# Index bits of a table look-up: GpSimd comparisons and subtractions replaced by VectorE int32 and-operations

## The chip, the core and the metric

One program runs on one core of a Trainium2 chip. The core's engines run side by side, each through its own list of instructions in order: TensorE (PE; its weight loads are shown apart as PEld), VectorE (DVE), ScalarE (ACT), GpSimd (POOL), and SyncE (SP), which here only issues DMAs. They are held together by semaphores: an instruction may wait until a semaphore has reached a number, and may raise one when it ends. The metric is the device time of the whole program in microseconds (us), lower being better.

## What is computed

Four layers of attention and feed-forward blocks run over activations of 4 batches x 256 rows x 256 columns. The change lies in the third layer (numbered 2), whose feed-forward block holds its weights as indices into a table of 16 numbers:

```python
def _ghost_linear(x, idx, lut):
    w = lut[idx]                      # lut: 16 floats, idx: int32 from 0 to 15
    return jnp.einsum('bsh,oh->bso', x, w)
gate = _ghost_linear(x, gate_idx, lut)    # 688 x 256 indices
up   = _ghost_linear(x, up_idx, lut)      # 688 x 256
...
return _ghost_linear(h, down_idx, lut)    # 256 x 688
```

Before it comes that layer's cross attention: 16 heads of width 16, 4 batches of 256 queries, keys split into main and extra ones. The kernel computes the weights `w = lut[idx]` of the feed-forward block while this attention runs.

## The kernel before

**The look-up.** All indices of the layer lie in one tile `w2` (in `regD`) of 128 partitions x 4288 words, loaded as int32 and replaced in place by float weights. It is cut into 8 pieces (`LUT_PIECES`) of LP = 536 words. For each piece the index b3 b2 b1 b0 is split into bits, and a binary tree of selections is walked:

- GpSimd (lines 593 to 607) turns the int32 indices into floats (`left`, line 601), then for 8, 4 and 2 writes a mask m = bit if left >= bit else 0 (line 603) and subtracts it (line 604). What is left is b0 as a float (`lut_b0`). That is 7 instructions a piece and 56 in all, each waiting for the one before (`link`). Two sets of buffers alternate, so piece i waits until the 7 selections of piece i - 2 are done (`lut_pick`). It signals `lut_bits`.
- ScalarE (`lut_leaves`, lines 954 to 963) makes 8 leaves lut[2k] + b0 (lut[2k+1] - lut[2k]), two instructions in each of four steps k. Each step waits for `lut_bits`, later ones also for selections that free a buffer. It signals `lut_leaf`. The first leaf is written over the indices in `w2`.
- VectorE (`lut_step`, lines 1605 to 1625) selects between leaves with 7 predicated copies (`choose`, line 1611), by m1 (bit 2), m2 (bit 4) and m3 (bit 8).

**Where it sits.** The attention runs over b = 0 to 3 and h = 0 to 15; I number its 64 steps i = 16 b + h. In a step TensorE forms the shifted scores of head i (lines 2207 and 2208), the plain scores of a head of the next batch (line 2187, in steps h = 3 to 12 of b = 0 to 2), and the values of head i - 1 (line 2223). Both scores of a head are written to one of two banks, so TensorE's line 2187 waits until VectorE has taken the row maxima of the head two before. VectorE takes these maxima (lines 1573 and 1574), ScalarE the exponentials (line 977), VectorE normalises four heads at a time (lines 1592 to 1598) in steps h = 2, 6, 10, 14. Once in a batch VectorE splits the 32 maxima of each head and row into three bf16 parts (lines 1581 to 1584) for TensorE's line 2194, which ScalarE copies out (line 952).

**The order** is written by hand. Piece p of the look-up has seven steps; its step s stands in attention step i = 5 + 7 p + s (`LUT_START, LUT_STEPS = 5, 7`). ScalarE makes leaves in steps 1 to 4, VectorE selects in steps 2 to 6, so step 0 is empty on both engines. In VectorE's list the look-up stands behind the maxima of the same attention step and ahead of the normalising. GpSimd has nothing else to do between the layer norms before and behind the attention (`ln_pow`, lines 449 to 452). The feed-forward block behind the attention, `ffn(1)`, waits for all 56 selections.

## Time and profile before

| | us |
|---|---|
| median of 3 runs | 1039.76 |
| lowest and highest | 1039.58 and 1040.32 |
| the profiled execution | 1043.5 |
| its span in the trace | 1042.0 |

The profile is of one execution. Its times count from the span's start, and the attention with the look-up lies between 708 and 866 us. An instruction's duration runs from its start to its end; on one engine the next one may start a little before the end of the one before, when it waits for nothing.

| profile of the stretch 700 to 866 us | |
|---|---|
| predicated copies of the look-up (VectorE, line 1611) | 56, busy 54.08 us |
| leaves of the look-up (ScalarE, line 962) | 64, mean 0.82 to 0.83 us |
| GpSimd's masks and subtractions (lines 603, 604) | 24 and 24, median 2.0 and 1.3 us |
| granted TensorE clock, mean | 0.89 |

### The profile page before, as it was taken

The numbers are of one execution on the slowest core, as the hardware profiler recorded it, in microseconds if no ns is written. First come the engines' busy times: TensorE is split into PE (matmuls) and PEld (weight loads), VectorE is DVE, ScalarE is ACT, GpSimd is POOL, SyncE is SP. The second block draws the span as 40 slices with busy tenths as digits, with TensorE's granted clock in tenths as the row PEclk, the third lists the DMA queues.
The fourth block names the chain that finished last, engine by engine and source line by source line (L and its number), as shares of the span: only waits on it lengthen the run. The fifth ranks groups of instructions, "written<-read, shape, count | busy, mean of one in ns | idle before, by whom it ended". The sixth has DMA issues, their size and how long they took to land.

```text
span 1042.0 us, 13075 instructions
## 1 busy us (share of the span) xinstructions
PE 875.7 (84%) x4352; PEld 618.7 (59%) x4352; DVE 719.4 (69%) x1377; ACT 533.1 (51%) x983; POOL 444.4 (43%) x274
## 2 busy tenths in 40 slices
PE   5795999999999997645669896958688799999998
PEld 3354777787787776423344553727477685545646
DVE  5247789989899997689856757745989873353311
ACT  2485687787777877622312524535587572112120
POOL 2011678878788785654630002005467540600000
PEclk8898899999999998966869998967699999999999
DMA  4003000000000000003120000000000001200000
GB/s 124 16 6 131 16 17 22 23 15 15 15 15 30 18 1 6 1 0 157 39 82 0 1 1 0 1 1 1 1 2 2 1 1 35 94 0 1 11 10 21
DMA packets 12923, 24.25 MB, mean 23 GB/s; under 512 B 4280, under 2 KB 8656, under 8 KB 11728
## 3 DMA queue, kind: packets, MB, share of 16 engines
q1 hardware_dynamic: 12448, 20.53, 6.0%
q10 hardware_dynamic: 432, 3.15, 0.8%
q8 instruction: 26, 0.43, 0.2%
q14 instruction: 17, 0.14, 0.0%
HBM read 22.63 MB, written 1.05 MB: 23 GB/s over the span
## 4 chain that ended last, share of the span: by engine, by line
PE 30%; DVE 17%; issue 5%; ACT 4%; POOL 1%; ACTq 0%; DVEq 0%
PE PS L2120 12%; PE PS L2169 6%; PE PS L2223 3%; DVE mxf L1573 2%; DVE regD L1611 1%; PE PS L2024 1%; PE PS L1673 1%; DVE regB L1611 1%; DVE regA L1323 1%; PE PS L2000 1%; DVE mx_am L1274 1%; PE PS L2187 1%; PE PS L2038 1%; PE PS L2207 1%; PE PS L1946 1%
## 5 line engine op out<-in xcount | busy, mean ns | idle before, releaser
L483 POOL TENSOR_TENSOR X<-X,xn 128x512 f32<-128x512 f32 x64 | 108.1, 1689 | 75.7 <-ACT xn L701 75.0
L451 POOL TENSOR_SCALAR veps<-mv 128x4 f32<-128x4 f32 x16 | 5.5, 346 | 266.7 <-DVE mv L1023 266.7
L1122 DVE TENSOR_TENSOR_SCAN regB<-regB 128x1024 f32<-128x1024 f32 x32 | 84.4, 2641 | 0.2
L1103 DVE TENSOR_SCALAR_CACHE_REDUCE regA<-PS,nrq 128x256 bf16<-128x256 f32 x128 | 56.0, 475 | 38.0 <-PE PS L1748 36.1
L720 ACT ACTIVATE regA<-PS,nb,rq 128x256 f32<-128x256 f32 x128 | 72.0, 574 | 13.5 <-DVE regA L1103 12.7
L2223 PE MATMUL PS<-regA 128*128 128x128 f32 x512 | 74.8, 293 | 3.4 <-ACT regA L977 3.3
L477 POOL TENSOR_TENSOR y<-y,regB 128x1024 f32<-128x1024 f32 x32 | 75.5, 2362 | 3.9 <-DVE regB L1133 3.8
L1770 PE MATMUL PS<-regA 128*128 128x256 f32 x256 | 67.6, 387 | 7.3 <-DVE qss L1090 7.2
L2223 PEld LDWEIGHTS PS<-regA 128*128 128x128 f32 x512 | 68.2, 206 | 7.1 <-ACT regA L977 6.1
L1779 PE MATMUL PS<-regA 128*128 128x256 f32 x256 | 68.4, 391 | 1.1 <-ACT xn L701 1.1
L1748 PE MATMUL PS<-regA 128*128 128x256 f32 x256 | 68.3, 390 | 0.0
L1721 PE MATMUL PS<-xnT,regA 128*128 128x512 f32 x128 | 60.6, 616 | 4.6 <-ACT regA L692 3.4
L2120 PE MATMUL PS<-xnT,regB 128*128 128x512 f32 x128 | 61.1, 628 | 1.3 <-ACT xnT L632 1.3
L2169 PE MATMUL PS<-regB 128*128 128x256 f32 x256 | 58.7, 387 | 3.6 <-DVE X L1550 3.5
L916 ACT ACTIVATE regB<-PS 128x512 f32<-128x512 f32 (+1 forms) x28 | 16.7, 596 | 84.1 <-PE PS L2120 84.0
L2120 PE MATMUL PS<-regA,regB 128*128 128x512 f32 x128 | 55.8, 594 | 1.4 <-ACT regA L906 1.4
L701 ACT ACTIVATE xn<-PS,ls 128x256 f32<-128x256 f32 x128 | 54.3, 487 | 5.0 <-DVE ls L1109 2.4
L2169 PEld LDWEIGHTS PS<-regB 128*128 128x128 f32 x256 | 49.2, 194 | 12.6 <-DVE X L1550 4.3
L1770 PEld LDWEIGHTS PS<-regA 128*128 128x128 f32 x256 | 47.5, 193 | 14.7 <-DVE qss L1090 8.4
L1779 PEld LDWEIGHTS PS<-regA 128*128 128x128 f32 x256 | 50.2, 197 | 8.7 <-issue 1.4
L1748 PEld LDWEIGHTS PS<-regA 128*128 128x128 f32 x256 | 46.5, 195 | 14.8 <-issue 9.6
L726 ACT COPY regA<-PS 128x512 f32<-128x512 f32 x64 | 38.0, 595 | 29.6 <-PE PS L1759 29.6
(271 smaller groups left out, 2164.4 us busy)
## 6 DMA issues: line engine op xcount, KB each, us to landing
regA<-in_W SPq DMA_DIRECT2D x16, 384.0 KB, 3.0
regB<-in_wg SPq DMA_DIRECT2D x2, 1024.0 KB, 6.3
regB<-in_wu SPq DMA_DIRECT2D x2, 1024.0 KB, 8.4
X<-in_x SPq DMA_DIRECT2D x1, 1024.0 KB, 7.8
regC<-in_wg ACTq DMA_DIRECT2D x1, 1024.0 KB, 5.7
regC<-in_wu ACTq DMA_DIRECT2D x1, 1024.0 KB, 7.9
regC<-in_wd ACTq DMA_DIRECT2D x1, 1024.0 KB, 9.9
regB<-in_wd SPq DMA_DIRECT2D x1, 1024.0 KB, 9.0
```

What stands on the lines that cost most here:

```text
L477: pool.tensor_tensor(halves(y3, i), halves(y3, i), halves(prod, i), ALU.add).then_inc(y_done, 1)
L483: pool.tensor_tensor(xt, xt, xh0[b % 2], ALU.add).then_inc(x0_add, 1)
L720: act.activation(p0[i][:, q, :], bank(S_BANK + i)[:, q * S:(q + 1) * S], ACT.Exp, bias=nb0[:, i, q:q + 1], scale=rq[par][:, 2 * b + q:2 * ...
L1103: ins = dve.tensor_scalar(spill[:, i, q, :], bank(S_BANK + i)[:, q * S:(q + 1) * S], nrq[par][:, t:t + 1], None, ALU.mult, ALU.min, accum_ ...
L1122: dve.tensor_tensor_scan(v(hs), v(dA), v(dBu), 0.0, ALU.mult, ALU.add).then_inc(scan_done, 1)
L1721: last = pe.matmul(to[:, i * HALF:(i + 1) * HALF], w0[par][:, c * P:(c + 1) * P], xnT[:, c, i * HALF:(i + 1) * HALF], start=c == 0, stop=c ...
L1748: last = pe.matmul(bank(S_BANK + b % 2)[:, q * S:(q + 1) * S], qT[par][:, (2 * b + q) * P:(2 * b + q + 1) * P], kT[par][:, b * S:(b + 1) * S],
L1770: last = pe.matmul(bank(O_BANK)[:, 0:S], ctxN[:, 2 * b + k, :], pT0[b % 2][:, k, :], start=k == 0, stop=k == 1)
L1779: last = pe.matmul(bank(W_BANK)[:, q * DIM:(q + 1) * DIM], oT0[b % 2][:, q * P:(q + 1) * P], wvo[par], start=True, stop=True)
L2120: last = pe.matmul(bank(to)[0:rows, :], w[:, k, c * P:c * P + rows], src[:, k, :], start=k == 0, stop=k == KD - 1)
L2169: last = pe.matmul(bank(6 + td % 2)[:, 0:DIM], hT[0:rows, c, t * P:(t + 1) * P], wd[0:rows, c, :], start=c == 0, stop=c == nch - 1)
L2223: last = pe.matmul(bank(6 + g % 2)[:, at:at + P], pT2[i % 3][:, k, q * P:(q + 1) * P], V2flat[:, v:v + P], start=k == 0, stop=k == 1)
```

## The change

GpSimd's loop goes away whole. The formerly empty step 0 of each piece on VectorE gets four instructions that read the int32 indices and write the bits 2, 4, 8 and 1 as int32, by `bitwise_and` with a constant. The masks are read as words that are zero or not, so an int32 2 serves as well as a float 2.0. ScalarE now reads b0 as int32 0 or 1 in place of a float. The three masks raise a semaphore of their own, `lut_mask`, for which the first selection waits; b0 raises `lut_bits`, for which ScalarE waits as before. The waits for free buffers move to VectorE's list.

```diff
-            pool.wait_ge(ld_i2, 16 * 5)
-            pool.wait_ge(stk_out, 4 * B)
-            for i in range(LUT_PIECES):
-                left = lut_b0[i % 2]
-                if i == 1:
-                    pool.wait_ge(q2_mm, 4)
-                if i >= 2:
-                    pool.wait_ge(lut_pick, 7 * (i - 1))
-                link(pool.tensor_copy(left, w2[:, i * LP:(i + 1) * LP].bitcast(I32)))
-                for m, bit in zip(lut_m[i % 2][::-1], (8.0, 4.0, 2.0)):
-                    link(pool.tensor_scalar(m, left, bit, bit, ALU.is_ge, ALU.mult))
-                    ins = pool.tensor_tensor(left, left, m, ALU.subtract)
-                    if bit > 2:
-                        link(ins)
-                ins.then_inc(lut_bits, 1)
...
-                    last = act.activation(dst, lut_b0[i % 2], ACT.Identity, scale=lutd[:, leaf:leaf + 1], bias=lut[:, 2 * leaf:2 * leaf + 1])
+                    last = act.activation(dst, lut_b0[i % 2].bitcast(I32), ACT.Identity, scale=lutd[:, leaf:leaf + 1], bias=lut[:, 2 * leaf:2 * leaf + 1])
...
             def lut_step(i, step):
 
                 A = w2[:, i * LP:(i + 1) * LP]
+                if step == 0:
+                    if i == 1:
+                        dve.wait_ge(q2_mm, 4)
+                    if i >= 2:
+                        dve.wait_ge(lut_pick, 7 * (i - 1))
+                    for m, bit in zip(lut_m[i % 2], (2, 4, 8)):
+                        dve.tensor_scalar(m.bitcast(I32), A.bitcast(I32), bit, None, ALU.bitwise_and).then_inc(lut_mask, 1)
+                    dve.tensor_scalar(lut_b0[i % 2].bitcast(I32), A.bitcast(I32), 1, None, ALU.bitwise_and).then_inc(lut_bits, 1)
...
-                        dve.wait_ge(lut_bits, i + 1)
+                        dve.wait_ge(lut_mask, 3 * i + 3)
```

Three places in the lists of instructions show what moves. Names such as regB or xnT are the large regions in which the tiles lie; `[waits ...]` names the semaphores. Line numbers behind line 590 are 15 lower in the changed kernel until line 1593, and 7 lower from the look-up's selections on (1611 becomes 1604).

VectorE at piece 1 (b = 0, h = 12 and 13), before: from the maxima of the last head to the first selection.

```order
L1573 TENSOR_REDUCE mxf<-PS 128x2 [waits s2_mm]
L1574 TENSOR_REDUCE mxf<-PS 128x2
L1581 CAST mxs<-mxf 128x2x32 [waits mx_tr,max2]
L1582 TENSOR_TENSOR mxr<-mxf,mxs 128x64 [waits dve_chain]
L1583 CAST mxs<-mxr 128x2x32 [waits dve_chain]
L1584 TENSOR_TENSOR mxs<-mxr,mxs 128x2x32 [waits dve_chain]
L1611 COPY_PREDICATED regD<-xnT,regC 128x536 [waits lut_leaf,lut_bits]
```

The same place in the changed kernel.

```order
L1558 TENSOR_REDUCE mxf<-PS 128x2 [waits s2_mm]
L1559 TENSOR_REDUCE mxf<-PS 128x2
L1599 TENSOR_SCALAR xnT<-regD 128x536 [waits q2_mm]
L1599 TENSOR_SCALAR xnT<-regD 128x536 x2
L1600 TENSOR_SCALAR regC<-regD 128x536
L1566 CAST mxs<-mxf 128x2x32 [waits mx_tr,max2]
L1567 TENSOR_TENSOR mxr<-mxf,mxs 128x64 [waits dve_chain]
L1568 CAST mxs<-mxr 128x2x32 [waits dve_chain]
L1569 TENSOR_TENSOR mxs<-mxr,mxs 128x2x32 [waits dve_chain]
L1604 COPY_PREDICATED regD<-xnT,regC 128x536 [waits lut_leaf,lut_mask]
```

The four and-operations now stand between the last maxima and the split of the maxima. The same four stand at piece 3 (b = 1, h = 10) between maxima and normalising: first before, then after.

```order
L1573 TENSOR_REDUCE mxf<-PS 128x2
L1574 TENSOR_REDUCE mxf<-PS 128x2
L1592 RECIPROCAL rl<-PS 128x16
L1596 TENSOR_TENSOR regC<-PS,rl 128x2x64
L1597 TENSOR_TENSOR regC<-PS,rl 128x128
```

```order
L1558 TENSOR_REDUCE mxf<-PS 128x2
L1559 TENSOR_REDUCE mxf<-PS 128x2
L1599 TENSOR_SCALAR xnT<-regD 128x536 x3
L1600 TENSOR_SCALAR regC<-regD 128x536
L1577 RECIPROCAL rl<-PS 128x16
L1581 TENSOR_TENSOR regC<-PS,rl 128x2x64
L1582 TENSOR_TENSOR regC<-PS,rl 128x128
```

GpSimd, before: the end of the layer norm ahead of the attention, and the first of eight such pieces.

```order
L451 TENSOR_SCALAR veps<-mv 128x4
L452 TENSOR_TENSOR rstd<-veps,neghalf 128x4
L601 CAST regD<-regD 128x536
L603 TENSOR_SCALAR regB<-regD 128x536
L604 TENSOR_TENSOR regD<-regD,regB 128x536
L603 TENSOR_SCALAR regB<-regD 128x536
L604 TENSOR_TENSOR regD<-regD,regB 128x536
```

In the changed kernel GpSimd goes straight from one layer norm to the next, with nothing in between.

## Rows read from the trace of the kernel before

**Rows 1.** The page: busy time by engine, then the span in 40 slices.
```profile
PE 875.7 (84%) x4352; PEld 618.7 (59%) x4352; DVE 719.4 (69%) x1377; ACT 533.1 (51%) x983; POOL 444.4 (43%) x274
...
DVE  5247789989899997689856757745989873353311
```

**Rows 2.** Waits, 690 to 870 us: who waited for whom, us in total, times, longest.
```profile
PE PS L2187 <- DVE mxf L1574: 24.8, 18, 4.9
PE PS L2194 <- DVE mxs L1584: 6.2, 4, 2.1
ACT regA L977 <- PE PS L2208: 28.4, 23, 6.5
DVE mxf L1573 <- PE PS L2187: 13.7, 11, 4.7
```

**Rows 3.** Chain that ended last, 680 to 880 us: start, us, what (pieces picked out).
```profile
732.76 1.75 DVE regD L1611
...
754.25 0.88 DVE mxs L1581
...
793.01 1.89 DVE regD L1611
...
807.22 1.86 DVE regD L1611
...
841.29 1.84 DVE regB L1611
843.15 1.04 DVE regD L1611
```

**Rows 4.** GpSimd's two operations by line: duration in ns (min/median/max), first and last start.
```profile
L603 POOL TENSOR_SCALAR regB<-regD x12: 2003/2014/2580, 710.3 to 824.5; 128x536 f32<-128x536 f32 x12
L604 POOL TENSOR_TENSOR regD<-regD,regB x12: 1316/1322/1328, 712.4 to 827.0; 128x536 f32<-128x536 f32 x12
```

**Rows 5.** VectorE's predicated copies (line 1611) alone: stretch, length, busy (count), PEclk.
```profile
700.00:866.00 166.00, 54.08 (x56) 0.89 0.00 1
```

**Rows 6.** Timeline of VectorE, then of GpSimd: start us, us, what.
```profile
790.93 0.61 DVE L1581 CAST mxs<-mxf 128x64 bf16<-128x64 f32 x1
...
792.21 0.77 DVE L1611 COPY_PREDICATED regB<-xnT,regC 128x536 f32<-128x536 uint32 x1
793.01 1.88 DVE L1611 COPY_PREDICATED regD<-xnT,regB 128x536 f32<-128x536 uint32 x1
...
790.36 2.51 POOL L603 TENSOR_SCALAR regB<-regD 128x536 f32<-128x536 f32 x1
792.96 1.32 POOL L604 TENSOR_TENSOR regD<-regD,regB 128x536 f32<-128x536 f32 x1
```

**Rows 7.** Int32 and-operations of VectorE elsewhere by line, then its start-to-start spacing (timeline).
```profile
L1178 DVE TENSOR_SCALAR regA<-regC x6: 672/673/674, 149.0 to 370.1; 128x1024 int32 x6
L1275 DVE TENSOR_SCALAR mx_am<-mx_am x10: 180/181/1695, 454.2 to 519.6; 128x32 int32<-128x32 int32 x10
...
693.36 0.65 DVE L1573 TENSOR_REDUCE mxf<-PS 128x2 f32<-128x480 f32 x1
693.93 0.18 DVE L1574 TENSOR_REDUCE mxf<-PS 128x2 f32<-128x32 f32 x1
```

**Rows 8.** Timeline of ScalarE at pieces 1, 2 and 7: start us, us, what [idle before].
```profile
753.03 0.83 ACT L962 ACTIVATE regD<-regC,lut,lutd 128x536 f32<-128x536 f32 x1
...
756.64 0.37 ACT L952 COPY regB<-PS 96x256 bf16<-96x256 bf16 x1 [1.57 <-PE PS L2194]
...
767.90 0.82 ACT L962 ACTIVATE regD<-regD,lut,lutd 128x536 f32<-128x536 f32 x1
...
849.83 0.82 ACT L962 ACTIVATE regD<-regC,lut,lutd 128x536 f32<-128x536 f32 x1
```

**Rows 9.** Timeline of VectorE where the and-operations land: start us, us, what [idle before].
```profile
753.47 0.65 DVE L1573 TENSOR_REDUCE mxf<-PS 128x2 f32<-128x480 f32 x1
...
803.04 0.66 DVE L1573 TENSOR_REDUCE mxf<-PS 128x2 f32<-128x480 f32 x1 [1.72 <-PE PS L2187]
...
818.93 0.69 DVE L1419 TENSOR_TENSOR X<-X,regC 128x512 f32<-128x512 f32 x1 [1.59 <-PE PS L2072]
...
839.43 0.90 DVE L1611 COPY_PREDICATED regD<-regB,regC 128x536 f32<-128x536 uint32 x1 [3.71 <-ACT regC L962]
```

**Rows 10.** Timeline of ScalarE in b = 2: the leaf ahead of the 811 us selection.
```profile
809.91 0.82 ACT L962 ACTIVATE regC<-regD,lut,lutd 128x536 f32<-128x536 f32 x1
```

More of the change, by code:

```diff
@@ L312, in build @@
                              "o2_norm", "co_tr", "coT_done", "wo2_mm", "wo2_add"))
-        lut_bits, lut_leaf, lut_pick, sx_done, z_done, z_tr, z_add, bf_done, hw_mm, wd3_done, hs3_done, xh_mm, xh_out = (
-            sem(n) for n in ("lut_bits", "lut_leaf", "lut_pick", "sx_done", "z_done", "z_tr", "z_add", "bf_done", "hw_mm", "wd3_done",
+        lut_bits, lut_mask, lut_leaf, lut_pick, sx_done, z_done, z_tr, z_add, bf_done, hw_mm, wd3_done, hs3_done, xh_mm, xh_out = (
+            sem(n) for n in ("lut_bits", "lut_mask", "lut_leaf", "lut_pick", "sx_done", "z_done", "z_tr", "z_add", "bf_done", "hw_mm", "wd3_done",
                              "hs3_done", "xh_mm", "xh_out"))
```

## The prediction

> **What bounds the kernel now.** I read the page first. TensorE is the busiest engine over the span, and GpSimd, from which the work is taken, the idlest of the four [rows 1]. Averages over the span say little here, so I turned to the stretch of the attention, 708 to 866 us. Its waits show a ring: TensorE's plain scores wait 24.8 us for VectorE's maxima and its line 2194 6.2 us for the split maxima, while ScalarE's exponentials wait 28.4 us for TensorE and VectorE waits 13.7 us for TensorE [rows 2]. No row of ScalarE or VectorE waits for GpSimd's bits. The chain of waits goes through VectorE in long runs from 727 to 836 us, and then through TensorE and ScalarE. VectorE is what paces b = 0 to 2, since there it has maxima for the next batch to take. In b = 3 it has none, and there ScalarE and TensorE pace.
>
> So GpSimd's loop is never waited for, and taking it off GpSimd is worth nothing by itself. The change is decided by what it does to VectorE, in two ways of opposite sign.
>
> **What is taken away: a slowing of VectorE.** The 56 selections are equal in size. Undisturbed ones take 0.75 to 0.77 us, but many take far more. At 793.01 one takes 1.88 us, having started 0.05 us behind a GpSimd subtraction of 1.32 us; the one at 792.21, beside a GpSimd mask operation, takes 0.77 [rows 6]. The excess of the first, 1.13 us, is close to the subtraction's length, 1.32 us in nearly all of its rows, while mask operations vary from 2.00 to 2.58 [rows 4]: the selection seems to wait until GpSimd's subtraction has finished. Together the 56 take 54.08 us [rows 5]; 56 x 0.757 is 42.4, so the excess is 11.7 us. Other small instructions are struck too: the cast at 754.25 takes 0.88 against 0.20 undisturbed [rows 3], that at 790.93 0.61 [rows 6], a third 0.30 too much, 1.4 us together.
>
> The Trainium skill, "SBUF — State Buffer", section "SBUF: two separate sides", says that VectorE instructions with two SBUF inputs and GpSimd ones that read SBUF take one port pair in turn, for a whole instruction. By that rule all of the excess ends with GpSimd's loop. It would also make a selection that starts beside a mask operation wait for its end, and the 0.77 us at 792.21 [rows 6] does not bear that out. If only the stretches at subtractions were the loop's doing, the sum below would have 1.3 us less of gain.
>
> How much of the excess lies on the chain? I went through it piece by piece. Six stretched selections are off it (759.53, 770.07, 794.79, 796.87, 839.43, 845.09), with 3.5 us of excess. The rest is 11.7 - 3.5 = 8.2 us of selections, from 732.76 to 843.15 [rows 3], and 1.4 us of casts: **9.6 us**. Not all of it will be passed on:
> - Around 807 us ScalarE works without a gap. The selection at 811.6 needs the leaf that starts at 809.91 and lasts 0.82 [rows 10], so it can't move ahead by all of the 1.86 us gained before it and only by about 0.9. I take 1.0 us off.
> - The last two, at 841.29 and 843.15 [rows 3], have 1.36 us of excess. ScalarE had waited for them only 0.61, so 0.75 comes off.
>
> **What is added: 32 and-operations on VectorE.** The kernel has such instructions elsewhere: int32 of 1024 columns takes 673 ns, of 32 columns 181 ns undisturbed [rows 7]. On the line between them 536 columns take 181 + 504 x 492 / 992 = 431 ns. Nothing is waited for between the four, and then VectorE starts the next instruction some 0.08 us before the end of the last (693.36 + 0.65 against 693.93) [rows 7]. A group of four is 3 x 0.35 + 0.43, less 0.08 at the end: **1.4 us**. Bounds are the two rows themselves, 4 x 0.1 and 4 x 0.6 us. All eight groups are 11.2 us of VectorE, about the 11.7 + 1.4 that it gets back. It is the places that decide:
> - Piece 0 (721.3 us) falls where VectorE soon waits 0.8 and then 2.8 us for TensorE: nothing.
> - Piece 1 stands behind the maxima of 753.47 [rows 9], with VectorE solid behind it: 1.4.
> - Piece 2 (767.2) has 0.85 us of VectorE's idle time behind it in three small gaps: 0.55.
> - Piece 3 (786.6) is in a solid run: 1.4.
> - Piece 4 (800.2) has the gap of 1.72 behind it, piece 5 (817.2) that of 1.59, piece 6 (835.7) that of 3.71 [rows 9]: nothing. The gaps are waits for TensorE or ScalarE; if those came earlier by as much as VectorE does, they would stay as they are.
> - Piece 7 (849.1) is in b = 3, where VectorE has time: nothing on VectorE.
>
> **What is moved: ScalarE now waits for VectorE.** The leaves of a piece need its bits. GpSimd had them ready long before; now they come from VectorE's list one attention step earlier, and VectorE is the engine that lags. At piece 1 the leaves start at 753.03 [rows 8], while the and-operations can't end before 754.1 + 1.4 = 755.5, or 754.5 after the 1.0 us gained at 732.76. ScalarE starts them 1.4 us late, has the 1.57 us of idle time ahead of 756.64 [rows 8] to take that up, and is held back behind it only through VectorE's split maxima; where it becomes the chain at 761 us, some 0.4 of the 0.6 us won there (1.4 added, 1.0 and 1.0 removed) is lost: 0.4. At piece 2 (leaves at 767.90, bits at 768.4) the lateness is within the 0.55 already counted. At piece 7 the bits come at 850.5, the leaf was at 849.83 [rows 8]; TensorE has an output projection of 1.7 us to do in between, which covers most of it, so I put down 0.2. At the others the bits are in time.
>
> ScalarE reads int32 now. No row of before shows that on ScalarE. Its operation runs at one column after another at 0.82 us whatever region it reads, and the nearest row with int32 on another engine, VectorE's, shows no extra cost [rows 7], so I take 0, with 64 x 0.1 us as the upper bound. The waits on `lut_pick` and `lut_mask` in VectorE's list are for its own, finished work: nothing. GpSimd's layer norm behind the attention is not held up by its loop before either, which ended at 846 us.
>
> **The sum.** -9.6 + 1.0 + 0.75 + 1.4 + 0.55 + 1.4 + 0.4 + 0.2 = -3.9 us, on the profiled execution's 1043.5. That one stands 3.7 above the median of the runs, of which nothing is due to this stretch; so on the median 1039.8 - 3.9 = **1035.9 us**. One thing is left to luck: the granted clock in this stretch averages 0.89 [rows 5], and falls after TensorE's idle times; the output projection at 815.9 us takes 2.99 where its like takes 1.73 at 850.6. One such fall more or less is 1.3 us.
>
> **The rivals.**
>
> *VectorE gives back more (1031).* The and-operations find gaps everywhere and the stretches return in full: -9.6 - 1.3 (one slow projection less) + 1.4 + 0.6 = -8.9. For it: the gaps behind pieces 4 to 6 did take their groups whole. Against: ScalarE has no gap around 762 to 775 and 801 to 811 us.
>
> *The gain is hidden (1039.3).* As VectorE speeds up, ScalarE with its 64 leaves of 0.82 and TensorE take over the pace at each stretch, and of 9.6 us only half is passed on, 4.8, against 4.3 us of costs: -0.5. For it: three engines are each busy for 70 to 90% of this stretch. Against: TensorE waited 31 us for VectorE in it [rows 2], which says that VectorE is the late one.
>
> *ScalarE waits for its bits (1043.5, slower).* The mechanism is VectorE's list: bits for piece p stand behind VectorE's backlog of step 5 + 7 p. By the times of the trace leaves would come 2.5 us late at piece 1, 0.7 at piece 2, 0.9 at piece 3 and 0.6 at piece 7, 4.7 us together; exponentials queue behind the leaves on ScalarE, and TensorE's values wait for these. If nothing takes that up, and half of the stretches is passed on, it is -4.8 + 3.4 + 4.7 + 0.4 = +3.7. It decides from the point where lateness exceeds ScalarE's slack ahead of its next wait, 1.57 us at piece 1. The same time would come of and-operations at the speed of a 512-column addition (0.69 us each), or of an int32 input that costs ScalarE 0.1 us each.
>
> *The change does not do what it says* would be stretches that stay with GpSimd silent; then VectorE only gains work, +3.4 to +4: it is in the chance of the slower case.
>
> **Chances.** Forecast 1035.9, with its own range of 1033 to 1038: 0.50. More given back: 0.11. Hidden: 0.18. Slower: 0.21. About 0.2%, 2.1 us, is what a measurement of this kernel can tell from no change. The forecast's range and the first rival are faster, 0.61; hidden is the same, 0.18; the last is slower, 0.21. The range that leaves out 0.2 runs from inside the first rival to inside the last: 1031.0 to 1042.5.
>
> **What would show it.** VectorE's selections all at 0.75 to 0.77 us, total about 42.5; and-operations at 0.43; VectorE's busy time in the stretch about the same as before. ScalarE's line 962 with waits for the and-operations of at most 2 us at pieces 1 and 2. TensorE's 24.8 us of waiting for maxima down by 3 or more. The forecast is wrong if the selections stay stretched, if ScalarE's leaves show waits of more than 4 us for the and-operations in total, or if they take longer with an int32 input.

## The result, and the profile after

| | before | changed |
|---|---|---|
| median of 10 runs, us | 1040.59 | 1034.82 |
| lowest and highest, us | 1039.19 and 1043.02 | 1033.01 and 1037.80 |
| ratio to before, 95% interval | | 0.9942 [0.9930, 0.9955] |
| profiled execution, its span, us | 1043.5, 1042.0 | 1034.1, 1032.5 |

The change makes the kernel faster by 5.8 us. The forecast was 1035.9 on 1039.8, a gain of 3.9 us. The time lies within the forecast's 1033 to 1038; 1.9 us of the gain were not foreseen, and the experiments below are mostly about them.

The page of the changed kernel, in answer to [rows 1]: 32 more instructions on VectorE and yet a little less busy time (716.0 us for 719.4); GpSimd lost 86.5 us.

```profile
PE 866.4 (84%) x4348; PEld 613.4 (59%) x4352; DVE 716.0 (69%) x1409; ACT 532.3 (52%) x983; POOL 357.9 (35%) x218
```

The and-operations by line: duration min/median/max in ns, first and last start. The forecast had 431 ns.

```profile
L1599 DVE TENSOR_SCALAR regB<-regD x12: 422/431/434, 718.2 to 828.3; 128x536 int32<-128x536 int32 x12
L1600 DVE TENSOR_SCALAR regC<-regD x4: 432/438/446, 751.1 to 839.7; 128x536 int32<-128x536 int32 x4
```

The selections alone, in the stretch of [rows 5]: stretch, length, busy and count, granted clock. They are down from 54.08 us to 42.46, 0.758 each. The clock of the stretch, the last number but two, rose from 0.89 to 0.94, for which the forecast had no term.

```profile
700.00:866.00 166.00, 42.46 (x56) 0.94 0.00 1
```

The waits of 690 to 870 us, as in [rows 2]: who waited for whom, us in total, times, longest.

```profile
PE PS L2180 <- DVE mxf L1559: 23.4, 19, 4.9
PE PS L2187 <- DVE mxs L1569: 5.4, 3, 2.3
ACT regA L962 <- PE PS L2201: 23.7, 22, 4.1
DVE mxf L1558 <- PE PS L2180: 12.0, 6, 5.4
```

TensorE's waits for maxima fell by 1.4 us only, where 3 or more were forecast. The longest wait of an exponential fell from 6.5 to 4.1 us.

**A better ruler than the whole time.** The first exponential starts between 704 and 710 us in the profiles of this study (708.7 and 707.4 in two of the kernel before, 705.7 and 706.8 in two of the changed one). From the start of the first exponential to that of the last, the same kernel repeats itself within 0.1 us. The exponentials by line, kernel before, then changed (first and last start stand behind the durations):

```profile
L977 ACT ACTIVATE regA<-PS x64: 572/592/617, 708.7 to 862.5; 128x512 f32<-128x512 f32 x64
```

```profile
L962 ACT ACTIVATE regA<-PS x64: 573/592/613, 705.7 to 853.1; 128x512 f32<-128x512 f32 x64
```

Before, 153.8 us; changed, 147.5. A second profile of each gave 153.8 and 147.5. Of the 9.5 us between the two spans 6.3 belong to the attention, and some 3 to an earlier start, which varies by as much between profiles and lies ahead of everything that the change touches. So the gain to be explained is **6.3 us** (the medians say 5.8, within the interval of 4.7 to 7.3). I call this distance the attention time, and the start of exponential i, counted from the first, its offset.

The offsets say where the gain arises. The forecast of each stretch is made of the terms of the sum, and of the excess of the selections that start in it.

| steps i | offset at its end, before | the same, changed | gain in it | forecast |
|---|---|---|---|---|
| to 32 (pieces 0 to 3) | 88.2 | 87.8 | 0.4 | 0.6 |
| 32 to 40 (piece 4) | 104.8 | 103.7 | 0.7 | 0.8 |
| 40 to 41 | 111.9 | 108.4 | 2.4 | 0.6 |
| 41 to 47 (piece 5) | 126.4 | 120.6 | 2.3 | 1.8 |
| 47 to 48 | 128.6 | 121.9 | 0.8 | 0 |
| 48 to 63 (pieces 6, 7) | 153.8 | 147.5 | -0.3 | 0.4 |

The selection at 811.60 counts from step 40 to 41, since the maxima that TensorE waits for there stand behind it. The forecasts add up to 4.2 rather than 3.9, since the single excesses on the chain come to 8.5 where I had taken the rest of the total, 8.2. Two single steps, 40 to 41 and 47 to 48, hold 3.2 us of gain, of which 0.6 was forecast. The rest agrees with the sum to within 0.7 us at each line.

### The profile page after: what moved, and what is told of

Its sections match the earlier page's. It is cut to its first block, busy times and chain, and to the rows that moved or that the text cites. A ratio compares the mean times of both kernels' runs of the same rounds, so it can differ in the third digit from the quotient of the medians.

```text
span 1032.5 us, 13046 instructions
## 1 busy us (share of the span) xinstructions
PE 866.4 (84%) x4348; PEld 613.4 (59%) x4352; DVE 716.0 (69%) x1409; ACT 532.3 (52%) x983; POOL 357.9 (35%) x218
## 3 DMA queue, kind: packets, MB, share of 16 engines
q10 hardware_dynamic: 432, 3.15, 0.8%
HBM read 22.63 MB, written 1.05 MB: 23 GB/s over the span
## 4 chain that ended last, share of the span: by engine, by line
PE 29%; DVE 17%; ACT 5%; issue 5%; POOL 1%; ACTq 0%; DVEq 0%
PE PS L2113 12%; PE PS L2162 6%; PE PS L2216 3%; DVE mxf L1558 2%; PE PS L1666 1%; PE PS L2017 1%; PE PS L1993 1%; DVE mx_am L1259 1%; DVE regA L1308 1%; PE PS L2031 1%; ACT regC L947 1%; DVE regA L1286 1%; PE PS L2180 1%; DVE xn L1017 1%; PE PS L2200 1%
## 5 line engine op out<-in xcount | busy, mean ns | idle before, releaser
L477 POOL TENSOR_TENSOR y<-y,regB 128x1024 f32<-128x1024 f32 x32 | 77.6, 2427 | 0.7 <-DVE regB L1118 0.6
L2216 PEld LDWEIGHTS PS<-regA 128*128 128x128 f32 x512 | 65.8, 200 | 6.9 <-ACT regA L962 5.8
L1763 PEld LDWEIGHTS PS<-regA 128*128 128x128 f32 x256 | 47.9, 194 | 14.8 <-DVE qss L1075 8.4
L1772 PEld LDWEIGHTS PS<-regA 128*128 128x128 f32 x256 | 50.3, 197 | 8.7 <-issue 1.4
L1741 PEld LDWEIGHTS PS<-regA 128*128 128x128 f32 x256 | 46.0, 193 | 14.6 <-issue 9.5
```

The source lines that it names most:

```text
L477: pool.tensor_tensor(halves(y3, i), halves(y3, i), halves(prod, i), ALU.add).then_inc(y_done, 1)
L1741: last = pe.matmul(bank(S_BANK + b % 2)[:, q * S:(q + 1) * S], qT[par][:, (2 * b + q) * P:(2 * b + q + 1) * P], kT[par][:, b * S:(b + 1) * S],
L1763: last = pe.matmul(bank(O_BANK)[:, 0:S], ctxN[:, 2 * b + k, :], pT0[b % 2][:, k, :], start=k == 0, stop=k == 1)
L1772: last = pe.matmul(bank(W_BANK)[:, q * DIM:(q + 1) * DIM], oT0[b % 2][:, q * P:(q + 1) * P], wvo[par], start=True, stop=True)
L2216: last = pe.matmul(bank(6 + g % 2)[:, at:at + P], pT2[i % 3][:, k, q * P:(q + 1) * P], V2flat[:, v:v + P], start=k == 0, stop=k == 1)
```

## What stands behind the two steps: TensorE's clock

TensorE of the kernel before, timeline: start us, us, what, idle time before it and its releaser.

```profile
815.52 0.38 PE L2187 MATMUL PS<-regA,regB 96*128 96x256 bf16 x2 [1.99 <-DVE mxf L1574]
815.74 3.15 PE L2072 MATMUL PS<-regC,regB 128*128 128x256 f32 x8
...
832.62 0.28 PE L2194 MATMUL PS<-identb,mxs 128*96 128x128 bf16 x2 [2.08 <-DVE mxs L1584]
...
834.90 1.91 PE L2223 MATMUL PS<-regA 128*128 128x128 f32 x8
```

Two stretches behind them (stretch, length, busy and count on PE, PEld, DVE, ACT, POOL, then the granted clock):

```profile
817.00:819.00 2.00, 2.00 (x7) 1.65 (x6) 0.41 (x3) 0.00 (x0) 1.91 (x2) 0.50 0.00 0
...
833.30:836.60 3.30, 3.30 (x17) 2.98 (x17) 2.32 (x6) 0.60 (x2) 1.70 (x2) 0.50 0.00 0
```

Line 2072 is the output projection, line 2223 the values of a head. Behind each wait of some 2 us the clock is at 0.50, that is 1.2 GHz; I call such a stretch a spell. The projection in the first takes 3.15 us, the eight matmuls of the values in the second 1.91. The same places in the changed kernel, timeline and stretches:

```profile
810.62 0.38 PE L2180 MATMUL PS<-regA,regB 96*128 96x256 bf16 x2 [1.25 <-DVE mxf L1559]
810.84 1.89 PE L2065 MATMUL PS<-regC,regB 128*128 128x256 f32 x8
...
824.52 0.28 PE L2187 MATMUL PS<-identb,mxs 128*96 128x128 bf16 x2 [1.21 <-DVE mxs L1569]
```

```profile
812.00:814.00 2.00, 2.00 (x17) 1.85 (x16) 2.00 (x7) 0.00 (x0) 0.00 (x0) 1.00 0.00 0
...
826.00:828.00 2.00, 2.00 (x20) 1.95 (x19) 1.93 (x7) 1.04 (x2) 0.00 (x0) 1.00 0.00 0
```

The waits are 1.25 and 1.21 us, the clock stays at 1.00 (2.4 GHz), the projection takes 1.89 us, and the values take 1.06 (at 826.02). The forecast had seen the projection of 3 us and put it down to luck. A second profile of the kernel before, the run below, says that it was none.

> The kernel before once more, for a second profile. If its two spells of TensorE's lower clock (granted 0.50 at 817 to 819 us, 0.57 at 833 to 837 us, both behind a wait of 2.0 to 2.1 us) follow from the waits, they stand at the same steps of the attention again, and the attention takes 153.8 us from first to last exponential, within 0.3. If they are luck, they stand elsewhere or nowhere.

```profile
814.25 0.38 PE L2187 MATMUL PS<-regA,regB 96*128 96x256 bf16 x2 [1.98 <-DVE mxf L1574]
814.47 3.14 PE L2072 MATMUL PS<-regC,regB 128*128 128x256 f32 x8
...
831.32 0.28 PE L2194 MATMUL PS<-identb,mxs 128*96 128x128 bf16 x2 [2.07 <-DVE mxs L1584]
...
833.56 1.91 PE L2223 MATMUL PS<-regA 128*128 128x128 f32 x8
```

The attention took 153.8 us again, and both spells stand in the same places with the same lengths. They belong to the kernel.

Not every spell costs something. A third one, the longest, lasts from 734.3 to 751.3 us in the kernel before, 17 us at 0.50. In the changed kernel 10 us are left of it, yet at step 15, behind it, the offsets of the two kernels differ by 0.1 us only. So about half of the rise of the mean clock from 0.89 to 0.94 says nothing of the gain, and a spell has to be priced at its place.

To price the two I kept the kernel before, with GpSimd's loop, and gave TensorE something to do in the two waits: 16 transposes of a constant tile, which take 0.9 us of a wait, into a bank that is free there.

```diff
+                        if b == 2 and h == WO2:
+                            pe.wait_ge(stk_out, 4 * 2 * B)
+                            pe.wait_ge(wo2_add, 1)
+                            fill()
                         for hn in first_pass(b, h):
                             scores(b + 1, hn)
...
+                            if b == 2:
+                                fill()
...
+            def fill():
+                for n in range(16):
+                    pe.transpose(bank(0).bitcast(BF16)[:, (n % 8) * P:(n % 8 + 1) * P], identb[:, :], identb[:, :])
```

> The kernel before, with 16 transposes of a constant tile (some 0.9 us of TensorE, results not read) ahead of each of the two waits of b = 2 behind which its clock fell: in step i = 40 ahead of the plain scores and in step i = 46 ahead of line 2194. GpSimd's loop, the stretched selections and VectorE's list are as before. Theory A (part of the gain is the clock, which falls behind an idle spell of 2.0 us and not behind 1.2): both spells are gone, and the attention is 2.5 to 3 us shorter, 151 us, ratio 0.997. Rival (the clock falls for another reason, or the time is lost elsewhere): spells stay or the attention stays at 153.8 us; ratio 1.000 or above.

Measured: median 1038.15 of 7 runs, ratio 0.9974 [0.9963, 0.9984], attention 150.3 us. TensorE's timeline:

```profile
810.39 1.06 PE L2230 MATMUL PS<-identb 128*128 128x128 bf16 x16
...
812.54 0.38 PE L2187 MATMUL PS<-regA,regB 96*128 96x256 bf16 x2 [1.09 <-DVE mxf L1574]
812.76 1.89 PE L2072 MATMUL PS<-regC,regB 128*128 128x256 f32 x8
...
822.39 0.38 PE L2187 MATMUL PS<-regA,regB 96*128 96x256 bf16 x2 [1.32 <-DVE mxf L1574]
823.27 1.74 PE L2223 MATMUL PS<-regA 128*128 128x128 f32 x8
...
828.46 0.28 PE L2194 MATMUL PS<-identb,mxs 128*96 128x128 bf16 x2
```

The projection is back at 1.89 us, with VectorE up to there as in the kernel before (the selection ahead of it takes 1.33 us in both). Of the gain of 3.5 us, 1.7 arise from step 40 to 41 and 0.8 from 47 to 48, where the spells were, 0.3 between them and 0.7 behind them. The rows of the kernel before say the same of the two steps: the projection is 1.26 us longer than at the full clock and the values behind it 0.46 (1.51 for 1.05), together 1.7; at the second spell the values are 0.41 longer (1.52 for 1.11) and the four score matmuls 0.42 together, 0.8.

Two things keep this run from being a test of the clock alone. A new spell appeared at 823.5 us, behind a wait of 1.32 us. And the transposes shifted VectorE against GpSimd: behind the first place fewer selections are stretched, so that the 56 take 51.00 us in all instead of 54.08.

```profile
700.00:866.00 166.00, 51.00 (x56) 0.91 0.00 1
```

The selections at 823.33 and 827.26 of the kernel before, 1.71 and 1.63 us, take 0.75 and 0.77 here, and the wait ahead of line 2194 is gone whole. The 0.3 and 0.7 us outside the two steps may come from there. What is shown: **work added to TensorE in two waits makes the kernel faster, by a ratio of 0.9974 against the changed kernel's 0.9942, and the first of the two places by 1.7 us through the clock alone.** Taken place by place, the clock is worth 1.7 + 0.8 = 2.5 us of the 6.3, and 6.3 - 2.5 = 3.8 is what the forecast's own terms had to give, against the 3.9 it said.

Waits of 1.25 and 1.21 us in the changed kernel were followed by the full clock, and a wait of 1.32 us by the full clock in one kernel (`ands_to_3` below, at 826.20) and by a spell in this one. So the length of the last wait alone does not tell which wait is followed by a fall; what does, I leave open.

## Experiments on the forecast's own terms

My theory (A in the texts below) was that of the forecast, with rival ones named in each text.

**The changed kernel again**, as a floor for what a difference means.

> The changed kernel itself, run beside the others, so that they can be held against it. Ratio to the kernel before 0.994 within 0.001 by every theory. If the faster output projection (1.73 us where the kernel before took 2.99) is luck of one execution, this profile may show 2.99 again; if it follows from TensorE's shorter wait ahead of it, it shows 1.73.

Median 1035.0 of 6 runs, ratio 0.994 [0.9922, 0.9959]; attention 147.5 us.

**The and-operations left out.** Their price within the changed kernel.

```diff
-                if step == 0:
+                if step == 0 and i < 2:
...
-                        dve.wait_ge(lut_mask, 3 * i + 3)
+                        dve.wait_ge(lut_mask, min(3 * i + 3, 6))
```

> The changed kernel with the and-operations of pieces 0 and 1 alone; pieces 2 to 7 select by the bits of pieces 0 and 1, so their weights are wrong and 24 and-operations are left out. Theory A (each group of four costs its 1.4 us where VectorE paces, nothing where it has a gap): pieces 2, 3 and 5 are on the chain, with ScalarE's late leaves on top, so 3 to 4 us below the changed kernel, ratio to the kernel before about 0.9905. Rival B (the groups are hidden by ScalarE, which is the pace once GpSimd is silent): within 1 us of the changed kernel, 0.9935.

Median 1031.64, ratio 0.9901 [0.9883, 0.992], attention 144.2 us. So the 24 and-operations of pieces 2 to 7, with the late leaves that they cause, cost 3.2 us of attention. The offsets name the places: 0.5 us of it has arisen at step 24, which is piece 2, and 1.4 between steps 24 and 32, which is piece 3; the forecast had 0.55 and 1.4. Between 32 and 48 it grows by 0.3 only, for pieces 4 and 5 (forecast 0). The last 1.0 us arises in a single step, 48 to 49, and is piece 6's (forecast 0). Behind it nothing is added: piece 7 costs nothing (forecast 0.2).

**GpSimd busy again, with nobody waiting for it.** The changed kernel, with a loop of the old shape (a memset in place of the conversion, three mask operations, three subtractions, the same waits) on scratch tiles of GpSimd.

```diff
+            pool.wait_ge(ld_i2, 16 * 5)
+            pool.wait_ge(stk_out, 4 * B)
+            for i in range(LUT_PIECES):
+                if i == 1:
+                    pool.wait_ge(q2_mm, 4)
+                if i >= 2:
+                    pool.wait_ge(lut_pick, 7 * (i - 1))
+                link(pool.memset(scr0[:, :], 1.0))
+                for bit in (8.0, 4.0, 2.0):
+                    link(pool.tensor_scalar(scr1[:, :], scr0[:, :], bit, bit, ALU.is_ge, ALU.mult))
+                    link(pool.tensor_tensor(scr0[:, :], scr0[:, :], scr1[:, :], ALU.subtract))
```

> The changed kernel, and GpSimd runs a loop of the old shape on scratch that nobody reads: 8 pieces of one memset, three mask operations and three subtractions of 536 columns, with the old waits. Theory A (the gain is the end of GpSimd's stretching of VectorE): selections stretch to 1.8 us again, and the time is that of the kernel before plus the price of the and-operations, which now also can be stretched: ratio 1.002 to 1.005. Rival B (the gain came from GpSimd's bits being late, from the clock or from elsewhere): it stays at 0.994.

Median 1047.07, ratio 1.0058 [1.0039, 1.0076], attention 161.7 us: 14.2 us more than the changed kernel, by a loop whose result nobody reads. One group of selections by line (the rest look alike), min/median/max ns:

```profile
L1619 DVE COPY_PREDICATED ctxT<-regB,regC x4: 750/756/1890, 742.5 to 850.5; 128x536 f32<-128x536 uint32 x4
```

So the stretches are GpSimd's doing, and GpSimd's loop costs time without being waited for. The loss is larger than expected (1.002 to 1.005). It holds the slowed selections (50.8 us in all, durations added up, for 42.6 in the changed kernel), the slowed and-operations (18.7 for 13.9, some up to 1.54 us), and a clock of 0.87.

**Which of GpSimd's operations does it?** The same loop with the three subtractions alone, and with the three mask operations alone.

> The changed kernel, and GpSimd runs 24 subtractions of two 536-column scratch tiles (1.32 us each) with the old waits, three in a row per piece, and no mask operations. Theory A (a subtraction of GpSimd holds VectorE's two-input instructions up to its end): each selection or cast that starts beside one is stretched by up to 1.1 us; three in a row per piece are 4 us, in which some two selections start: 4 to 7 us of excess, half of it on the chain, ratio to the kernel before about 0.997. If any GpSimd operation stretches, gp_ts shows the same excess per busy microsecond; by theory A gp_ts shows a quarter of it or less.

> The changed kernel, and GpSimd runs 24 mask operations (one input tile, 2.0 us each) with the old waits, and no subtractions. Theory A: the mask operations themselves grow (to 2.4 us) and selections hardly, under 0.1 us in the mean; ratio to the kernel before 0.994 to 0.996. Rival (one port pair for whole instructions of any kind that read SBUF): selections and and-operations beside a mask operation wait for its end, up to 1.9 us each; 6 us or more of excess, ratio about 0.998 or above.

Both misses. The ratio with the masks is the one that its rival named (0.998 or above), but not by stretched selections. Subtractions alone: 1049.33, ratio 1.0072 [1.0053, 1.0091], attention 163.1 us. Mask operations alone: 1042.88 of 12 runs, ratio 1.001 [0.9995, 1.0025], attention 153.4 us. Hardly a selection was stretched: with subtractions the 56 took 42.6 us, the longest 0.78, with masks 42.7, the longest 0.92. What was stretched were the and-operations. The timeline with subtractions alone, VectorE and GpSimd:

```profile
764.87 4.19 POOL L605 TENSOR_TENSOR scr<-scr 128x536 f32<-128x536 f32 x3 [12.12 <-DVE regD L1617]
...
766.92 2.77 DVE L1612 TENSOR_SCALAR regB<-regD 128x536 int32<-128x536 int32 x3
```

And with mask operations alone:

```profile
767.12 6.33 POOL L605 TENSOR_SCALAR scr<-scr 128x536 f32<-128x536 f32 x3 [10.58 <-DVE regD L1617]
...
768.53 2.00 DVE L1612 TENSOR_SCALAR regB<-regD 128x536 int32<-128x536 int32 x3
```

Three and-operations take 2.77 and 2.00 us in place of 1.13. My scratch loops wait for the same selections (line 1617 there) as the group of and-operations behind them does. So without the alternation of two kinds of operation they run beside the group. With the subtractions they are over before the first selection; with the masks five selections still fall beside one. The lateness then goes on to ScalarE: its leaves waited 17.7 us in all for and-operations with the subtractions, 7.6 with the masks, 4.9 in the changed kernel. The longest such wait, with the subtractions, is 3.92 us, ahead of a leaf at 792.24.

The experiment did not separate the two kinds as I meant, since it moved the moment at which each ran. It shows something that I had not set out to find: a stretch is passed on whole where its victim is waited for. The largest price of GpSimd's work in this study, 15.7 us of attention, came with no selection stretched and 32 and-operations at 28.1 us in place of 13.9 (durations added up), an excess of 14.3. Not all of the price is theirs: both kernels also have three spells of 0.50 behind 752 us (at 756, 794 and 848 with the subtractions), where the changed kernel is at 1.00 until 853.

The Trainium skill, "SBUF — State Buffer", section "SBUF: two separate sides", says that a VectorE instruction in one of its faster, two-port modes and a GpSimd instruction exclude each other for a whole instruction, and so do a VectorE instruction with two SBUF inputs and a GpSimd one that reads SBUF. Beside subtractions the rows agree (and-operations of up to 1.56 us, selections of up to 1.89). Beside mask operations they don't. And-operations came to at most 0.88 us, though they started anywhere in a mask operation of 2.1 us. Selections are held in its first part alone. In the kernel before the one at 770.07 starts 0.09 us behind the mask operation and takes 1.16 us, as if it waited for 0.5 us of it and not for 2.0:

```profile
769.98 2.00 POOL L603 TENSOR_SCALAR xnT<-regC 128x536 f32<-128x536 f32 x1
...
770.07 1.16 DVE L1611 COPY_PREDICATED regD<-regB,regC 128x536 f32<-128x536 uint32 x1
```

Of the kernel before, those that start 0.94 us or more behind the start of a mask operation take 0.74 to 0.77, among them the one at 792.21 of [rows 6], 1.85 us behind.

**The and-operations twice.** Each group again, the second waiting for the first.

```diff
+                    for again in range(2):
+                      if again:
+                        dve.wait_ge(lut_mask, 6 * i + 3)
+                        dve.wait_ge(lut_bits, 2 * i + 1)
...
-                act.wait_ge(lut_bits, i + 1)
+                act.wait_ge(lut_bits, 2 * i + 2)
```

> The changed kernel with each group of four and-operations made twice (the second writes the same values over the first, and waits for it). Theory A: another 1.4 to 1.6 us a piece, on the chain at pieces 1, 2, 3, 5 and now partly 4, 6 and 7, with ScalarE's leaves later by as much: 8 us above the changed kernel, ratio to the kernel before about 1.002. Rival B (groups hidden behind ScalarE): up to 3 us above it, 0.997.

Median 1045.77 of 12 runs, ratio 1.0037 [1.0025, 1.0049], attention 157.6 us. That is more than the 8 us expected. 32 more and-operations cost 10.1 us, 0.32 each, where 24 fewer had brought 3.2, 0.13 each. The first group lies partly in gaps; the second finds fewer of them, and makes the leaves late (14.2 us of waits for bits against 4.9). The clock takes part too: spells of 0.50 stand at 754.5, 792.1 and 839.8 us, where the changed kernel has none. So the price of an instruction is no constant here: it more than doubles once the gaps are full.

**Which half of the change pays?** GpSimd's loop for pieces 0 to 3 and and-operations for 4 to 7, and the reverse.

```diff
+        BY_GPSIMD = range(0, 4)
...
+            for i in BY_GPSIMD:
+                left = lut_b0[i % 2]
...
-                if step == 0:
+                if step == 0 and i not in BY_GPSIMD:
```

> GpSimd's loop for pieces 0 to 3, and-operations for pieces 4 to 7. By the profiles the changed kernel is only 0.3 us ahead at step 32, where piece 4 begins, and 6.3 at the end. Theory A (stretching and clock falls of pieces 4 and 5 carry the gain): the attention takes 147.5 to 148.5 us, ratio to the kernel before 0.994 to 0.995. Rival (the gain of pieces 0 to 3 is real and handed on later): 151 us, ratio 0.997.

> And-operations for pieces 0 to 3, GpSimd's loop for pieces 4 to 7. Theory A: the attention takes 153 to 154 us, ratio to the kernel before 0.999 to 1.001. Rival: 151 us, ratio 0.997.

| | median us | ratio | attention us | against before |
|---|---|---|---|---|
| and-operations in pieces 4 to 7 | 1033.5 | 0.9929 [0.9916, 0.9942] | 146.5 | -7.3 |
| and-operations in pieces 0 to 3 | 1040.61 | 0.9993 [0.9977, 1.0009] | 154.6 | +0.8 |
| in all (the change) | 1034.82 | 0.9942 [0.993, 0.9955] | 147.5 | -6.3 |

Both lie outside what was expected (147.5 to 148.5, and 153 to 154). The two halves seem to add up, -7.3 + 0.8 = -6.5 against -6.3, but they are no clean halves: GpSimd runs ahead, and its loop for piece 4 begins at step 26, beside piece 3. By the offsets the first kernel is even with the kernel before up to step 24, wins 1.4 us by step 32, where that loop is missing, and from there to the end gains 6.0 us, as the whole change does. The second is even with the changed kernel up to step 24 and then loses 3.6 us by step 32: the loop for piece 4 meets piece 3's and-operations (one takes 0.86 us) and selections (up to 1.89), and a spell appears at 791.3. That loss neither the change nor the kernel before has. So and-operations made beside GpSimd's loop are the worst of both, and the 0.8 us is not the price of pieces 0 to 3. What the pair does show: the change's gain lies behind step 32, and GpSimd's loop for pieces 0 to 3 is 1.0 us faster than their and-operations, by the attention time; the whole times' intervals overlap.

The second of these kernels also bears out the part on the clock. It keeps GpSimd's loop for b = 2 and stretches such as this one of a selection beside a subtraction,

```profile
795.04 1.33 POOL L606 TENSOR_TENSOR regD<-regD,regB 128x536 f32<-128x536 f32 x1
795.09 1.89 DVE L1624 COPY_PREDICATED regD<-xnT,regB 128x536 f32<-128x536 uint32 x1
```

and has a wait of 1.41 us ahead of the projection, with the full clock behind it and 2.2 us gained on the kernel before in that step, but one of 2.38 us for the split maxima and slow work behind that:

```profile
816.35 0.38 PE L2203 MATMUL PS<-regA,regB 96*128 96x256 bf16 x2 [1.41 <-DVE mxf L1579]
816.57 1.89 PE L2088 MATMUL PS<-regC,regB 128*128 128x256 f32 x8
...
832.28 0.42 PE L2210 MATMUL PS<-identb,mxs 128*96 128x128 bf16 x2 [2.38 <-DVE mxs L1589]
832.49 2.02 PE L2239 MATMUL PS<-regA 128*128 128x128 f32 x8
```

**The groups in better places: a faster kernel.** If a group costs what it displaces, it can be put where VectorE waits anyway. Pieces 1 and 3 move to steps 11 and 23, between two instructions of the next batch's preparation (`stack_rest`), the second of which waits for ScalarE. Pieces 2 and 5 move to steps 17 and 34. All four are also earlier for ScalarE.

```diff
-            def stack_rest(b):
+            def stack_rest(b, bits=None):
...
+                if bits is not None:
+                    lut_bits_of(bits)
                 dve.wait_ge(stk_m, B + b + 1)
...
+            MOVED = {11: 1, 17: 2, 23: 3, 34: 5}
...
-                if step == 0:
+                if step == 0 and i not in MOVED.values():
+                    lut_bits_of(i)
...
+                    if i in (17, 34) and i in MOVED:
+                        lut_bits_of(MOVED[i])
...
-                        stack_rest(b + 2)
+                        stack_rest(b + 2, MOVED.get(i))
```

> The changed kernel with four groups of and-operations moved to where VectorE waits: piece 1 to step i = 11 and piece 3 to i = 23, each inside the wait of 1.1 us between the two subtractions of the query split; piece 2 to i = 17, ahead of a selection that waits 2.1 us for ScalarE; piece 5 to i = 34, ahead of a wait of 1.7 us for TensorE. Theory A: pieces 1 and 3 give back 1.1 each, piece 2 0.6, piece 5 1.0, and ScalarE's leaves no longer wait for bits: 3 us below the changed kernel, ratio to the kernel before about 0.991. Rival B (ScalarE and TensorE pace): within 1 us of the changed kernel.

> The changed kernel with only pieces 1 and 3 moved into the waits of the query split (i = 11 and 23). Theory A: 1.1 us each and the late leaves there: 2 us below the changed kernel, ratio to the kernel before about 0.992. Rival B: no difference, 0.994.

All four moved: median **1029.83** us, ratio 0.9899 [0.9878, 0.9921], attention 143.6 us. Pieces 1 and 3 alone: 1031.6, 0.99 [0.9881, 0.9919], 144.3 us. Both gave back about 1 us more than expected. The first beats both kernels, the changed one by 5.0 us of the medians and 3.9 of attention, and needs no more instructions; the two placed kernels' intervals overlap. In the changed kernel the instruction of `stack_rest` behind the moved group had waited:

```profile
748.11 0.69 DVE L1551 TENSOR_TENSOR regB<-regB 128x512 bf16<-128x512 f32 x1 [1.11 <-ACT regB L933]
```

With the groups moved that wait is filled, and the instruction starts without idle time behind the group (1.12 us for its first three):

```profile
745.73 1.12 DVE L1602 TENSOR_SCALAR xnT<-regD 128x536 int32<-128x536 int32 x3
747.12 0.68 DVE L1553 TENSOR_TENSOR regB<-regB 128x512 bf16<-128x512 f32 x1
```

ScalarE's leaves wait 1.2 us in all for their bits, not 4.9. With pieces 1 and 3 moved, 1.7 us were won on the changed kernel by step 15 and another 1.4 by step 32. So the group of piece 1 with its late leaves had cost at least 1.7 us (1.4 + 0.4 in the sum), and that of piece 3 at least 1.4, as `no_ands` says too.

## Why the prediction was right, point by point

**Right in the mechanism.** The stretches of selections end with GpSimd's loop and come back when a loop is put there that nobody reads, so the reason is shown and not only argued. The total of the selections is 42.46 us as forecast (42.5), and the int32 input costs ScalarE nothing:

```profile
L947 ACT ACTIVATE regC<-regD,lut,lutd x16: 818/822/844, 720.5 to 835.6; 128x536 f32<-128x536 int32 x16
```

**Right in the price of a group.** Piece 1 stands as forecast, 1.39 us from the first and-operation to the next instruction:

```profile
750.05 1.13 DVE L1599 TENSOR_SCALAR xnT<-regD 128x536 int32<-128x536 int32 x3
751.09 0.44 DVE L1600 TENSOR_SCALAR regC<-regD 128x536 int32<-128x536 int32 x1
751.44 0.19 DVE L1566 CAST mxs<-mxf 128x64 bf16<-128x64 f32 x1
```

**Right by halves on the late leaves.** They wait for bits where the forecast said, 2.17 us at piece 1 and 0.71 at piece 2, but also at pieces 3 and 6, which its own list had in time, and not at piece 7, which it had late. The rival's list (2.5, 0.7, 0.9 and 0.6 us at pieces 1, 2, 3 and 7) was the better one. ScalarE's timeline:

```profile
751.56 0.83 ACT L947 ACTIVATE regD<-regC,lut,lutd 128x536 f32<-128x536 int32 x1 [2.17 <-DVE regC L1600]
...
765.56 0.83 ACT L947 ACTIVATE regD<-regD,lut,lutd 128x536 f32<-128x536 int32 x1 [0.71 <-DVE regD L1600]
...
784.68 0.83 ACT L947 ACTIVATE regD<-regC,lut,lutd 128x536 f32<-128x536 int32 x1 [0.90 <-DVE regC L1600]
...
829.07 0.83 ACT L947 ACTIVATE regD<-regD,lut,lutd 128x536 f32<-128x536 int32 x1 [0.91 <-DVE regD L1600]
```

With 0.25 at piece 0 they total 4.9 us. The forecast said that more than 4 us would prove it wrong, and by that sign it is; the bound was badly set. Most of that waiting is slack, as its own 1.57 us at piece 1 says [rows 8]. The rival "ScalarE waits for its bits" had the mechanism and not the price: at piece 1 group and lateness together cost 1.7 us, near the 1.4 + 0.4 of the sum. Only at piece 6 did it cost more, as follows.

**Right on the gap of piece 4, wrong on those of pieces 5 and 6.** VectorE of the changed kernel:

```profile
812.35 1.13 DVE L1599 TENSOR_SCALAR xnT<-regD 128x536 int32<-128x536 int32 x3
813.73 0.69 DVE L1404 TENSOR_TENSOR X<-X,regC 128x512 f32<-128x512 f32 x1
...
830.73 0.77 DVE L1604 COPY_PREDICATED regD<-regB,regC 128x536 f32<-128x536 uint32 x1 [1.69 <-ACT regC L947]
```

The gap of 1.72 us [rows 9] stayed as it was behind piece 4 (1.74 ahead of the maxima at 799.62). That of 1.59 behind piece 5 is gone. It had been a wait for the slow projection, and with the projection at 1.89 us the group of piece 5 fills what is left. It cost little, since pieces 4 and 5 together were worth 0.3 us. The gap of 3.71 behind piece 6 is down to 1.69. It is a wait for a leaf, and that leaf now itself waits for the and-operations (0.91 us at 829.07, above); the next exponential stands behind it in ScalarE's list. A gap that ends with the reader of the added work does not take this work whole: the forecast's "they would stay as they are" fails there. Piece 6 cost 1.0 us, all in step 48 to 49, where 0 stood in the sum, and piece 7 nothing where 0.2 stood. That is what the last line of the table of offsets is short, -0.3 against 0.4.

**The term that was mis-sized: the clock.** The step reads "One thing is left to luck: the granted clock" and gives one fall as 1.3 us in either direction, outside the sum. The two spells stand in both profiles of the kernel before, they are gone in both of the changed one, and they are worth 2.5 us. Half of it was on record, the slow projection and that the clock falls after TensorE's idle times. The wait of 1.99 us ahead of it was there to be read, and a lead of VectorE was likely to shorten that wait; the projection's neighbour, the second spell, was missed. The rival "gives back more" had one spell less in it, for 1.3 us, and the gain came out near the middle between it and the forecast.

**Luck in the rest.** That 3.8 us remain where 3.9 were forecast is better than the terms deserve. The costs, measured one by one, are 1.7, 0.5, 1.4, 0.3 and 1.0 us for pieces 1, 2, 3, 4 with 5, and 6, that is 4.9 where the sum had 3.95. (The rival "hidden" puts these same costs at 4.3, which none of the terms gives.) So the part of the stretches that came back must have been about 0.9 us larger than the forecast's 7.85, which is argued and not measured by itself; the line of steps 41 to 47, 2.3 against 1.8 with piece 5's 0.3 us of cost in it, holds most of that.

**The forecast that failed beside it.** "TensorE's 24.8 us of waiting for maxima down by 3 or more": it fell to 23.4. The two waits ahead of the spells got shorter (1.99 to 1.25, 2.08 to 1.21), the longest stayed at 4.9. Where TensorE's own work became shorter it is done sooner and waits again elsewhere. That reading is argued from the rows and was not tried by itself. The total of an engine's waits was a poor sign of the gain.

What stays open: what exactly makes the clock fall behind one wait and not behind another; how the two operations of GpSimd share the blame, since the two loops that were to tell ran at other moments; and how the 0.3 and 0.7 us that the transposes won outside the two steps divide between fewer stretched selections and the clock. Not tried: pieces 0 to 3 on GpSimd together with moved groups for the others, and other places for pieces 6 and 7.

## What to carry to other kernels

An engine that nobody waits for can still cost time, by slowing its neighbour: compare equal instructions with and without it, and cost what comes back only where the slowed one is on the chain. Work put onto a lagging engine is paid by place. Look for a wait inside a pair of dependent instructions, ahead of the time at which the added work's reader needs it; the same 16 instructions moved by one to six steps were worth 3.9 us of attention here. And when TensorE runs slow behind a wait that the change will shorten, profile the kernel twice: if the slow spell is in the same place again, it belongs into the sum.

## What the runs showed of the hardware that I had not expected

- The clock's low spells are as repeatable as instructions: a projection of 3.15 and 3.14 us behind waits of 1.99 and 1.98 us in two profiles, 1.89 us behind waits of 1.09, 1.25 and 1.41. Transposes whose result is thrown away, 0.9 us of them in the wait, bring the full clock back there. With two such groups the kernel is 2.7 us faster [1.7, 3.8], some of which may be due to fewer stretched selections.
- The kinds of GpSimd's operations differ in whom they hold, and for how long. Beside subtractions of 1.3 us selections and and-operations are held up to their end, to 1.89 and 1.56 us. Beside mask operations of 2 us and-operations at most double, from 0.43 to 0.88, and selections take up to 1.20 us (in `gp_both`, at 756.43) when they start just behind the mask operation's start, and 0.74 to 0.78 when they start 0.94 us behind it or later.
